# Row maxima of the attention over 64 rows a head, two heads in two row groups, 500 keys a piece

## What is computed

```python
logits = jnp.einsum('bthd,bshd->bhts', q, k) * HD ** (-0.5)
causal = jnp.tril(jnp.ones((T, T), dtype=bool))
logits = jnp.where(causal, logits, -jnp.inf)      # in the temporal attention alone
att = jax.nn.softmax(logits, axis=-1)
o = jnp.einsum('bhts,bshd->bthd', att, v).reshape(B, T, D)
```

## Time and profile before

| what | us |
|---|---|
| median of the runs shown (3) | 1969.96 |
| lowest, highest of them | 1966.17, 3506.1 |
| the profiled execution, its own time | 1968.53 |
| its span, first to last instruction | 1966.7 |

### The profile page before, as it was taken

The page is one execution under the profiler, slowest core; times in us unless marked ns, Lnnn a source line. Parts: engine busy times, 40 slices in busy tenths (PEclk is TensorE's granted clock), DMA queues, the critical chain, the costliest instruction groups (busy, mean ns, idle before and its releaser), DMA issues.

```text
span 1966.7 us, 30993 instructions
## 1 busy us (share of the span) xinstructions
PE 1820.8 (93%) x10495; PEld 1624.1 (83%) x10495; DVE 1184.8 (60%) x2343; ACT 723.6 (37%) x1346; POOL 337.7 (17%) x335
## 2 busy tenths in 40 slices
PE   2999999986999999999989999989999999899998
PEld 1788567855899989889889898889999999787996
DVE  7776567775556546663756647656665666675332
ACT  1223211014655435445445554245545444220110
POOL 3210001002212011020100004100000013565440
PEclk9999999988999999999999999999999999999999
DMA  3101001011031000030000000000000001111101
GB/s 108 33 7 44 11 11 32 1 48 44 11 122 38 27 17 6 1 121 12 12 6 11 12 1 12 27 11 12 6 12 6 6 1 62 55 54 48 43 33 52
DMA packets 24783, 58.00 MB, mean 29 GB/s; under 512 B 2538, under 2 KB 4806, under 8 KB 24014
## 3 DMA queue, kind: packets, MB, share of 16 engines
q1 hardware_dynamic: 24650, 56.18, 8.8%
HBM read 44.87 MB, written 11.30 MB: 29 GB/s over the span
## 4 chain that ended last, share of the span: by engine, by line
PE 79%; DVE 12%; issue 3%; DMA 2%; ACT 1%; DVEq 1%; POOL 1%; SPq 0%; POOLq 0%; ACTq 0%
PE ps L2284 19%; PE ps L2169 13%; PE ps L2339 7%; PE ps L1961 6%; PE ps L2266 5%; PE ps L2270 5%; PE ps L2227 5%; PE ps L2368 4%; DVE max_part L1712 4%; PE ps L2055 3%; PE ps L2092 3%; DVE share L1729 2%; PE ps L1974 1%; PE ps L2295 1%; DMA tok_a<-in_x 1%
## 5 line engine op out<-in xcount | busy, mean ns | idle before, releaser
L2284 PE MATMUL ps<-p_raw,v_ones 125*128 125x250 f32 x2080 | 527.0, 375 | 10.5 <-DVE feat L1731 8.4
L1712 DVE TENSOR_REDUCE max_part<-ps 125x2 f32<-125x500 f32 x520 | 330.3, 674 | 236.8 <-PE ps L2227 224.4
L1288 ACT ACTIVATE p_raw<-ps 125x500 f32<-125x500 f32 x520 | 304.3, 586 | 351.3 <-PE ps L2270 346.7
L2284 PEld LDWEIGHTS ps<-p_raw,v_ones 125*128 125x128 f32 x2080 | 360.8, 190 | 37.1 <-issue 9.8
L1729 DVE RECIPROCAL share<-ps 64x250 f32<-64x250 f32 x120 | 206.3, 1719 | 75.5 <-PE ps L2284 72.5
L2266 PE MATMUL ps<-q_both_a,k_both_a 128*125 128x250 f32 x520 | 184.2, 374 | 1.8 <-issue 0.9
L2266 PE MATMUL ps<-q_both_b,k_both_b 128*125 128x250 f32 x520 | 181.8, 371 | 0.0
L1552 DVE TENSOR_SCALAR onehot<-iota_h,win_key,key_t 125x320 f16 x453 | 170.2, 376 | 0.7 <-issue 0.6
L892 POOL CAST w_hi<-w_raw 128x512 fp32r<-128x512 f32 x44 | 28.3, 643 | 825.2 <-issue 359.7
L2169 PE MATMUL ps<-xa_hi,w_hi 128*128 128x418 f32 (+1 forms) x448 | 150.2, 335 | 14.9 <-POOL w_lo L894 9.1
L1551 DVE TENSOR_SCALAR onehot<-iota_h,low_t 125x125 f16 x453 | 126.2, 279 | 59.5 <-PE ps L2092 30.8
(11 more groups left out here) (378 smaller groups left out, 3395.9 us busy)
## 6 DMA issues: line engine op xcount, KB each, us to landing
w_raw<-in_w_mlp SPq DMA_DIRECT2D x32, 256.0 KB, 2.6
w_raw<-in_w_gps SPq DMA_DIRECT2D x16, 256.0 KB, 2.6
w_raw<-in_w_tp SPq DMA_DIRECT2D x16, 256.0 KB, 2.6
w_raw<-in_w_sp SPq DMA_DIRECT2D x12, 256.0 KB, 2.7
w_raw<-in_w_cr SPq DMA_DIRECT2D x12, 256.0 KB, 2.6
d_xt<-xb_hi SPq DMA_DIRECT2D x1, 2508.0 KB, 7.5
d_xt<-xb_lo SPq DMA_DIRECT2D x1, 2508.0 KB, 14.9
xa_hi<-d_xt SPq DMA_DIRECT2D x1, 2508.0 KB, 9.6
```

The lines of the kernel that those rows point to most:

```text
L1288: act.activation(p_raw[:, g % PR, :], ps[0:TOK, g % 2, 0:4 * TOK], ACT.Exp, scale=SCALE).then_inc(s_exp, 1)
L1712: dve.tensor_reduce(part[:, y, :, j], ps[0:TOK, bank, 0:4 * TOK].rearrange("p (h k) -> p h k", h=2), AX.X, ALU.max)\
L2284: ins = pe.matmul(ps[:, bank, 0:2 * TOK], v_ones[:, n % 2, kt, h:h + 2, :], p_raw[:, g % PR, cols], start=(b == 0 and x == 0), stop=last)
```

## The change

A piece M now covers up to 500 keys. It uses the upper parts alone: head 0 over rows 0 to 63, head 1 over rows 64 to 127, each into a bank of its own, so that the two products lie in different row groups of the array. `pieces` replaces `blocks_in` in the count of pieces: 3 for five blocks. A masked last piece first does its unmasked 250 keys (if it has two blocks), then the masked 250 and the two mask products. M waits for `s_q_hi` and `s_k_hi`, which ScalarE gives when the upper parts are written, and the score product waits in its place for `s_q_lo` and `s_k_both`. A piece takes two neighbouring banks, 4 and 5 or 6 and 7. VectorE reduces both in one instruction of up to 2 x 500 elements. In the plan M is taken once a step, costs 0.4 in place of 0.24, and its due steps are one apart. The openings are cut to the new number of pieces. The core of the diff:

```diff
+def pieces(n, i):
+
+    return -(-blocks_in(n, i) // 2)
...
-    return [("M", n, i, y, j) for y in range(2) for j in range(blocks_in(n, i))]
+    return [("M", n, i, y, j) for y in range(2) for j in range(pieces(n, i))]
...
-COST = {"K": 2.3, "V": 2.3, "Q": 1.4, "M": 0.24, "R": 0.2, "T": 0.7, "F": 3.0}
+COST = {"K": 2.3, "V": 2.3, "Q": 1.4, "M": 0.4, "R": 0.2, "T": 0.7, "F": 3.0}
...
-                due[task] = gf - 5 - 2 * (len(tasks) - 1 - x) // 3
-            due["Q", n, i] = gf - 8 - 2 * len(tasks) // 3
+                due[task] = gf - 5 - (len(tasks) - 1 - x)
+            due["Q", n, i] = gf - 8 - len(tasks)
...
-                if task[0] in LINEAR and g < linear_at + 2 or used.count(task[0]) >= (2 if task[0] == "M" else 1):
+                if task[0] in LINEAR and g < linear_at + 2 or task[0] in used:
...
+        elif kind == "M":
+            free = [x for x in (4, 6) if not any(held.get(b, "-")[0] in "KQF" and at[held[b]] >= slot for b in (x, x + 1))]
+            first = min(free or [4, 6], key=lambda x: max(order.get(x, -1), order.get(x + 1, -1)))
+            use = [first, first + 1]
+            order[first] = order[first + 1] = len(banks)
...
-                dve.tensor_reduce(part[:, y, :, j], ps[0:TOK, bank, 0:4 * TOK].rearrange("p (h k) -> p h k", h=2), AX.X, ALU.max)\
-                    .then_inc(s_max_part, 1)
-                count = blocks_in(n, i)
+                width = 2 * TOK * min(2, blocks_in(n, i) - 2 * j)
+                dve.tensor_reduce(part[:, y, :, j], ps[0:TOK, bank:bank + 2, 0:width], AX.X, ALU.max).then_inc(s_max_part, 1)
+                count = pieces(n, i)
...
-                bank, tile, keys = BANKS["M", n, i, y, j][0], slice(TOK * y, TOK * y + TOK), slice(2 * TOK * j, 2 * TOK * (j + 1))
-                masked = CAUSAL[n // 4] and j == i
+                bank, tile = BANKS["M", n, i, y, j][0], slice(TOK * y, TOK * y + TOK)
+                first, count = 2 * j, min(2, blocks_in(n, i) - 2 * j)
+                masked = CAUSAL[n // 4] and first + count - 1 == i
                 left(("M", n, i, y, j))
-                pe.wait_ge(s_q_lo, 5 * n + i + 1)
-                pe.wait_ge(s_k_both, 3 * n + 3)
-                for h in range(2):
-                    to = ps[0:TOK, bank, 2 * TOK * h:2 * TOK * (h + 1)]
-                    ins = pe.matmul(to, q_both[h][:, ring(n, i), tile], k_both[h][:, n % 2, keys], start=True, stop=not masked)
-                    if masked:
-                        ins = pe.matmul(to, identb[0:TOK, 0:TOK], causal_mask[0:TOK, TOK * (1 - y):TOK * (3 - y)], start=False, stop=True)
+                pe.wait_ge(s_q_hi, 5 * n + i + 1)
+                pe.wait_ge(s_k_hi, 3 * n + 3)
+
+                def rows(at, width, last):
+
+                    for h, r in enumerate((slice(0, 64), slice(64, 128))):
+                        keys = slice(2 * TOK * first + at, 2 * TOK * first + at + width)
+                        ins = pe.matmul(ps[0:TOK, bank + h, at:at + width], q_both[h][r, ring(n, i), tile], k_both[h][r, n % 2, keys],
+                                        start=True, stop=last)
+                    return ins
+
+                if masked:
+                    if count == 2:
+                        rows(0, 2 * TOK, True)
+                    at = 2 * TOK * (count - 1)
+                    rows(at, 2 * TOK, False)
+                    for h in range(2):
+                        ins = pe.matmul(ps[0:TOK, bank + h, at:at + 2 * TOK], identb[0:TOK, 0:TOK], causal_mask[0:TOK, TOK * (1 - y):TOK * (3 - y)],
+                                        start=False, stop=True)
+                else:
+                    ins = rows(0, 2 * TOK * count, True)
                 ins.then_inc(s_max, 1)
...
                     pe.wait_ge(s_q_both, 5 * n + i + 1)
+                    pe.wait_ge(s_q_lo, 5 * n + i + 1)
                     if i == 0:
+                        pe.wait_ge(s_k_both, 3 * n + 3)
                         pe.wait_ge(s_k_lo, 3 * n + 3)
```

More of the change, by code:

```diff
@@ L160, in value_turns @@
     return [("T", n, b) for b in range(3)]
-OPENING = {n: [("K", n, 0), ("K", n, 1), ("K", n, 2), ("Q", n, 0), ("V", n, 0), ("V", n, 1)] + maxima(n, 0)[0:3] + [("V", n, 2)] + maxima(n, 0)[3:6]
-           + [("Q", n, 1)] + maxima(n, 0)[6:] + [("R", n, 0)] + value_turns(n)
+OPENING = {n: [("K", n, 0), ("K", n, 1), ("K", n, 2), ("Q", n, 0), ("V", n, 0), ("V", n, 1)] + maxima(n, 0)[0:2] + [("V", n, 2)] + maxima(n, 0)[2:4]
+           + [("Q", n, 1)] + maxima(n, 0)[4:] + [("R", n, 0)] + value_turns(n)
            for n in (0, 8)}
@@ L1791, in _ @@
                 query_lo(n, 0)
-                for task in largest[:6]:
+                for task in largest[:4]:
                     maximum(*task[1:])
                 query_lo(n, 1)
-                for task in largest[6:]:
+                for task in largest[4:]:
                     maximum(*task[1:])
```

## The result

| | median us | runs | ratio to before, 95% interval |
|---|---|---|---|
| before | 1968.44 | 5 | |
| changed | 1982.72 | 5 (1981.94 to 1984.71) | 1.0078, 1.0062 to 1.0094 |

The medians differ by 14.3 us. The prediction said 2020, 51 us above its own base. The direction and the range of 1980 to 2046 held. The size did not: at less than 2% this counts as "no change", where the text gave "slower" the largest chance (0.52 against 0.41). The time of the result is that of the rival *loads side by side* (1984).

The account below looks back on a forecast made before the run. TensorE was taken to bound the kernel, busy 93% of the span. Streams -26, visits +110, waits that go -35 and waits that come +2 gave +51 us, about 2020; own range 2000 to 2036, with first rivals 1980 to 2046.

Parts of the forecast that it names:

- loads side by side: Rival for M's pairs: the second head's weight loads while the first's does, 36 us less, 1984; chance 0.22.
- streams of M: TensorE's products of M: 121.7 us before, 95.4 us after in paired row groups, saving 26 us.
- 306 visits: Stretches of M products over 64 rows among ones over 128: 0.36 us each, +110 us, range 0 to 116.
- the middle: For M's pairs: heads stream together but weights load one after the other, saving 26 us, between bounds of 3 and 62.
- rows 5: Trace rows before the change: 31 products of two columns, 0.11 us apart, taken as the load of a 128-column weight.
- Waits that go: TensorE's waits at M, R and P for maxima, lower halves and feat shrink, together 35 us.
- early gate: M waits for upper halves written by ScalarE, not lower ones made by VectorE: 12 us of waits go.
- Waits that come: A piece of M holds two banks for 1.19 us, nearly covered by a 1.3 us slot: +2 us.
- pairs of banks: Rival: M pieces wait for each other's reductions on their banks, 27 us more, 2045; chance 0.10.
- Reductions: VectorE's maxima: 1.19 us for 1000 elements, 318 us in sum where there were 350.
- The pairs' distance: Sign: starts of a 500-key pair's two products about 0.11 us apart; near 0 means loads side by side, 0.23 no overlap.
- no overlap: Rival: the two products of an M pair run one after the other despite two groups, 22 us more, 2042; chance 0.12.

Follow-up runs that it names:

- pair issued twice: The changed kernel with every unmasked pair of products of M issued twice in a row into the same banks: 2032.1 us, ratio 1.0328.
- steps of equal content: Matching steps timed in the changed kernel with M waiting for lower halves and copied keys (1992.1 us) against the same kernel with M over 128 rows (1949.9 us).
- 128-row kernel: The changed kernel with each product of M over all 128 rows, heads one after the other, waiting for lower halves and copied keys: 1949.9 us, ratio 0.9908.
- two a step: Plan allowing two pieces M in a step: on the changed kernel 2028.1 us, ratio 1.0301; on the 128-row kernel 2027.8 us, ratio 1.0300.

## Why the prediction was right and wrong

| term | predicted | measured | from |
|---|---|---|---|
| streams of M | -26 | -62 | pairs of 0.226 and 0.117 (timeline, pair issued twice) |
| 306 visits | +110 | +116 | 0.385 each, 0.33 with a mask (steps of equal content) |
| waits that go, less those that come | -33 | -40 | not measured: what is left to 14.3 |
| sum | +51 | +14 | |

- **What bounds the kernel.** Right. In the attention of the changed kernel TensorE is busy 1209 of 1237 us, and what its products or its waits gained or lost is what the time moved by.
- **Streams: the step that failed.** "I take the middle since rows 5 are the only rows that show what a load costs." Rows 5 show the rate at which one and the same part of the array takes new weights. That two parts must share that rate was read into them. The loads of the two heads start 0.01 us apart, a pair of 250 columns costs 0.117 us and one of 500 costs 0.226, so 36 us more were saved than counted. This is the error of the forecast (51 - 36 = 15); the errors of the other two terms, +6 and -7, cancel. The Trainium skill, TensorEngine Tiling (Array Packing), Key Properties, has tiles load and multiply in parallel: the trace agrees. The rival built on it had a chance of 0.22 and gave 1984.
- **Changes of height.** Right in mechanism and size. The 33-row product gave 0.38 in and out; the 64-row pairs show 0.38 to 0.39 on the timeline, whether a linear layer or P stands behind them. Lowering it to 0.36 for P's sake had no ground: P takes its share of it, 0.11, at its own next step. Where the mask product (bf16) follows it is less, 0.33. The reading behind it, "the array empties first, twice", agrees with the 0.09 us by which each change of height comes late both ways (pair issued twice); that the array empties in this time is argued, since no record shows it. The Trainium skill, on the same page under Key Properties, names such a drain at a change of the tiling mode.
- **Waits that go.** Near in size, in part by luck. The early gate was priced at 12 and measured at 9.4; R fell from 19.1 to 9.3 (foretold: 8), P's wait for feat from 8.4 to 1.9. But the other parts foretold, 21 us net, came to 15 (18.3 us from before to the 128-row kernel, less 3 of stream; it holds plan, pieces and the lighter VectorE together). So 33 us foretold were some 24. Another 15 were not foretold: steps made longer by visits wait less (57 against 42 above). The parts make 9.4 + 15 + 15 = 39, which they must, since each is a difference of the same medians. The gain was largest in the causal passes, which the prediction didn't set apart.
- **Waits that come.** Right: 3.4 us for a bank, foretold under 5. One piece a step is what keeps it there; with two a step the rival *pairs of banks* is real, with most of 78 us.
- **Reductions.** 1.19 us foretold, 1.200 measured, and 318 us in sum in both.
- **Signs foretold.** The first product comes "some 0.3 us after": it was 0.21 with its own 0.10 of loading inside its record. The pairs' distance was named as the sign between the rivals, and it told: 0, not 0.11. The cross passes (8 to 11) took 391.3 us before and 409.2 after, 18 more where "some 20" was said. This is no support for the forecast's sum: with 36 us in all passes wrongly counted, some of it here, the agreement is partly luck. The waits there had little to give.
- **Small slips.** By the prediction's own terms no overlap would be 23 us more (2043) and pairs of banks 2047, and of the range 2000 to 2036 a quarter, not a third, lies under 2009. No conclusion hangs on them.

The best version of this study is the changed order with products over all 128 rows: 1949.9 us, 0.9% under the kernel before. The gain is with its wider pieces, its plan and its longer reductions taken together, and not with its row groups.

## What to carry to other kernels

Splitting the array by rows halves the time of the stream, but each time a split product stands among full ones TensorE starts late twice and its weight loads are not hidden; here that is 0.38 us, more than one pair of 500 columns saves (0.23). Split only where several pairs stand in a row and the banks and the engine behind can take them, or leave the full height and widen the pieces. A wait can cost more than its length, when the granted clock falls behind it. Price such a thing from any low product in the trace, read to the second instruction behind it, since P hides a part of the price in its own next step. And where two resources might be shared or not, a row that shows one in use doesn't tell; give the case of no sharing its full weight.

## What the runs showed of the hardware

- Weights for two row groups load at the same time: starts 0.00 to 0.01 us apart, while new weights for the whole array come 0.11 us apart.
- Two fp32r products in different row groups and banks run fully side by side at 500 and 250 columns: a further pair of 500 inside a visit costs 0.22 us (pair issued twice), as much as one product of 500 over all rows (0.23).
- Going from 128 rows to 64 and back costs 0.38 to 0.39 us with fp32r or fp32 products on both sides, 0.33 with a bf16 product behind: 0.09 of late start and 0.10 of unhidden load each way (pair issued twice). A height of 65 or 97 rows costs nothing; 33 does.
- The net price of the 64 rows is 57 us by the medians of the steps and 42 in the measured time; waits that shrink took up a part of the difference.
- Behind waits of TensorE the granted clock can fall to 0.50, and a product of 250 columns then takes 0.21 us instead of 0.12 (two pieces in a step, 128 rows, from 697.2 to 700.6 us).
